# Attention scores of a state-space layer: from four fp32 products a batch to split fp32r products of 256 columns

## The reference

```python
B_ssm = ssm_in[..., :64]; C_ssm = ssm_in[..., 64:128]
# per token t and head: h = exp(d_t*A)*h + X_t * (d_t*B_t);  y_t = h . C_t
```

## Time and profile before

| | us |
|---|---|
| median of 3 runs (1521.78 to 1521.9) | 1521.87 |
| the profiled execution | 1522.09 |
| its span in the trace | 1520.4 |
| TensorE busy | 1504.6 (99%) |
| VectorE, GpSimd, ScalarE busy | 1128.1, 655.8, 606.0 |

### The profile page before, as it was taken

The page is one execution under the profiler, slowest core; times in us unless marked ns, Lnnn a source line. Parts: engine busy times, 40 slices in busy tenths (PEclk is TensorE's granted clock), DMA queues, the critical chain, the costliest instruction groups (busy, mean ns, idle before and its releaser), DMA issues.

```text
span 1520.4 us, 25377 instructions
## 1 busy us (share of the span) xinstructions
PE 1504.6 (99%) x8630; PEld 1250.7 (82%) x8630; DVE 1128.1 (74%) x3186; ACT 606.0 (40%) x1376; POOL 655.8 (43%) x747
## 2 busy tenths in 40 slices
PE   8999999999999999999999999999999999999998
PEld 7778888888888878888888888888888888888876
DVE  7797676967768677686876769777686776868755
ACT  6752424425244351533525244252443515335130
POOL 6771634616245270643606346162451715436040
PEclk9999999999999999999999999999999999999999
DMA  5350312314023040321404123140231403214020
GB/s 170 109 162 22 121 41 68 102 29 138 17 80 92 28 139 15 105 72 46 122 14 125 45 65 105 29 131 24 74 95 30 139 15 99 77 42 125 18 77 7
DMA packets 81505, 114.55 MB, mean 75 GB/s; under 512 B 10168, under 2 KB 37344, under 8 KB 81376
## 3 DMA queue, kind: packets, MB, share of 16 engines
q1 hardware_dynamic: 81376, 112.93, 24.6%
HBM read 107.77 MB, written 5.13 MB: 74 GB/s over the span
## 4 chain that ended last, share of the span: by engine, by line
PE 93%; POOL 2%; DVE 2%; DMA 1%; issue 1%; ACT 0%; SPq 0%; POOLq 0%; DVEq 0%; ACTq 0%
PE exp_bank L253 23%; PE exp_bank L255 22%; PE exp_bank L254 22%; PE mix_bank L964 4%; PE mix_bank L920 4%; PE mix_bank L253 3%; PE mix_bank L255 3%; PE mix_bank L254 3%; PE mix_bank L933 3%; PE mix_bank L814 1%; PE mix_bank L545 1%; PE mix_bank L762 1%; PE mix_bank L1056 1%; PE mix_bank L524 0%; POOL Wt L881 0%
## 5 line engine op out<-in xcount | busy, mean ns | idle before, releaser
L1241 POOL TENSOR_TENSOR sp_lo<-fbuf,sp_hi 128x512 fp32r<-128x512 f32 (+2 forms) x201 | 243.2, 1214 | 169.5 <-ACT sp_hi L1237 104.2
L253 PE MATMUL exp_bank<-w_hi,sp_hi 128*128 128x512 f32 x768 | 303.9, 396 | 1.2 <-POOL sp_lo L1294 0.8
L253 PE MATMUL exp_bank<-sp_hi,w_hi 128*128 128x512 f32 x764 | 302.8, 396 | 0.8 <-POOL sp_lo L1241 0.7
L255 PE MATMUL exp_bank<-w_hi,sp_lo 128*128 128x512 f32 x768 | 299.8, 390 | 0.0
L254 PE MATMUL exp_bank<-w_lo,sp_hi 128*128 128x512 f32 x768 | 299.0, 389 | 0.0
L255 PE MATMUL exp_bank<-sp_hi,w_lo 128*128 128x512 f32 x764 | 297.8, 390 | 0.0
L254 PE MATMUL exp_bank<-sp_lo,w_hi 128*128 128x512 f32 x764 | 297.5, 389 | 0.0
L1345 DVE SCALAR_TENSOR_TENSOR acc<-exp_bank,dw,acc 128x128 f32<-128x128 f32 x384 | 132.4, 345 | 163.6 <-PE exp_bank L255 162.8
L1237 ACT CAST sp_hi<-fbuf 128x512 fp32r<-128x512 f32 (+2 forms) x203 | 120.0, 592 | 270.7 <-DVE fbuf L1207 214.5
L881 POOL TENSOR_TENSOR Wt<-Wt,Gh 128x512 f32<-128x512 f32 x128 | 185.3, 1449 | 29.9 <-DVE Wt L870 29.9
L579 POOL TENSOR_TENSOR delta<-delta,bias_b 128x32 f32<-128x32 f32 x16 | 4.0, 253 | 414.3 <-ACT delta L555 409.2
(11 more groups left out here) (276 smaller groups left out, 2228.1 us busy)
## 6 DMA issues: line engine op xcount, KB each, us to landing
row_b<-dw_rows SPq DMA_DIRECT2D x189, 256.0 KB, 3.3
seg_b<-dA_rows SPq DMA_DIRECT2D x125, 256.0 KB, 3.4
ctd<-cum_rows SPq DMA_DIRECT2D x128, 96.0 KB, 3.2
x_in<-in_x SPq DMA_DIRECT2D x16, 256.0 KB, 2.7
result<-acc SPq DMA_DIRECT2D x15, 256.0 KB, 2.2
fbuf<-in_W1T SPq DMA_DIRECT2D x12, 256.0 KB, 4.0
acc<-in_W2T SPq DMA_DIRECT2D x4, 256.0 KB, 3.5
x_in<-in_W2T SPq DMA_DIRECT2D x4, 256.0 KB, 2.8
```

The lines of the kernel that those rows point to most:

```text
L253: nc.tensor.matmul(ps, s_hi, m_hi, start=start and j == 0, stop=False, skip_group_check=onto)
L255: last = nc.tensor.matmul(ps, s_lo, m_hi, start=False, stop=stop and j == n - 1, skip_group_check=onto)
L1241: sig("xw_lo", on.tensor_tensor(lo[:, cols], wide[e % 2][:, cols], hi[:, cols].bitcast(F32), ALU.subtract))
```

## The change

From batch 2 on, the scores are computed from split halves. The high half of B (rows 0 to 63) and its low half (rows 64 to 127) are stacked in one tile BS; CS holds the high half of the doubled C and, side by side, its low half. One fp32r product per chunk with K = 128 and 256 columns gives (B_hi+B_lo) C_hi and (B_hi+B_lo) C_lo in two column halves, which VectorE adds while it reads them from PSUM (`tensor_reduce`). BS and CS lie in the memory of zg.

The scores are made in two uses of a bank, two chunks each: the first behind transpose and sums, the second behind the third of the four column blocks of `expert_in(p, 0)`. The order of uses from batch 2 on is X0, X1, rates, G01, G23, X2, zg0 and so on, 25 a batch: G01 waits for the copy of X1, G23 for "ends", X2 and zg0 for VectorE's two sums. ScalarE's copy of the scores goes; its copy of B goes to BS; it makes C's high half behind tanh, and GpSimd C's low half behind the early part of the split. VectorE makes B's low half behind C's copies. The running product comes behind both sums on VectorE, where it was behind the end-sum reduction.

```diff
+MIX_LATER = (
+    MIX_USES[:MIX_USE["G"]] + [("rates", "ends", 1), ("G01", "Gm2", 1), ("G23", "Gm2", 2)] + MIX_USES[MIX_USE["X2"]:]
+)
+MIX_LATER[MIX_USE["BC"]] = ("BC", "B_lo", 1)
...
+        BS = nc.alloc_sbuf_tensor_at("BS", [P, T], F32R, offset=zg_at)
+        CS = nc.alloc_sbuf_tensor_at("CS", [P, 2, T], F32R, offset=zg_at + 4 * T)
...
 mix_bc:
-                AC.copy(BT[0:NS, :], bank_of("BC", b)[0:NS, :])
+                if later(b):
+                    wait(AC, "ps_out", b.prev())
+                    sig("B_hi", AC.copy(BS[0:NS, :], bank_of("BC", b)[0:NS, :]))
+                else:
+                    AC.copy(BT[0:NS, :], bank_of("BC", b)[0:NS, :])
...
+            if eng is DVE and later(b):
+                wait(DVE, "BC", b)
+                wait(DVE, "B_hi", b)
+                sig("B_lo", DVE.tensor_tensor(BS[NS:2 * NS, :], bank_of("BC", b)[0:NS, :], BS[0:NS, :].bitcast(F32), ALU.subtract))
+
+        def mix_c_split(eng, b):
+            if eng is AC and later(b):
+                wait(AC, "BC", b)
+                wait(AC, "ps_out", b.prev())
+                sig("C_hi", AC.copy(CS[:, 0, :], CT[:, :]))
+            if eng is PO and later(b):
+                wait(PO, "C_hi", b)
+                sig("C_lo", PO.tensor_tensor(CS[:, 1, :], CT[:, :], CS[:, 0, :].bitcast(F32), ALU.subtract))
...
+        def mix_scores_half(eng, b, n):
+            use, cs = f"G{2 * n}{2 * n + 1}", slice(2 * n, 2 * n + 2)
+            if eng is PE:
+                wait(PE, "B_lo", b)
+                wait(PE, "C_lo", b)
+                ps = mix_bank(b, use)
+                for j in range(2):
+                    at = tok(2 * n + j)
+                    last = PE.matmul(ps[:, 2 * j * P:2 * (j + 1) * P].rearrange("p (k t) -> p k t", k=2), BS[:, at], CS[:, :, at],
+                                     start=True, stop=True)
+                sig("ps_G2", last)
+            if eng is DVE:
+                wait(DVE, "ps_G2", b, n + 1)
+                wait(DVE, "G_dt", b.prev())
+                sig("Gm2", DVE.tensor_reduce(Gm[:, cs, :], bank_of(use, b)[:, :].rearrange("p (c k t) -> p c t k", c=2, k=2), AX.X, ALU.add))
...
 body:
             if norm_before:
                 expert_split(eng, p, 0, [1])
-                mix_scores(eng, b)
                 mix_silu_split(eng, b)
                 mix_rates(eng, b)
                 mix_ends(eng, b)
+                mix_scores_half(eng, b, 0)
+                if eng is DVE:
+                    mix_scores_half(DVE, b, 1)
+                    mix_running_product(b)
...
-                expert_in(eng, p, 0)
+                expert_in(eng, p, 0, lambda hc: hc == 2 and mix_scores_half(PE, b, 1))
...
                 mix_z(eng, nxt)
                 if eng is AC:
+                    mix_c_split(AC, nxt)
                     AC.preload_act_table_set(LOG_EXP)
             expert_row(eng, b, 0)
             expert_split(eng, b, 0, [0])
+            if front_next and eng is PO:
+                mix_c_split(PO, nxt)
```

More of the change, by code:

```diff
@@ L47 @@
 MIX_USE = {u[0]: n for n, u in enumerate(MIX_USES)}
+MIX_LATER = (
+    MIX_USES[:MIX_USE["G"]] + [("rates", "ends", 1), ("G01", "Gm2", 1), ("G23", "Gm2", 2)] + MIX_USES[MIX_USE["X2"]:]
+)
+MIX_LATER[MIX_USE["BC"]] = ("BC", "B_lo", 1)
+LATER_USE = {u[0]: n for n, u in enumerate(MIX_LATER)}
 MIX_FIRST = (
@@ L194, in layer_program @@
         product("G_skip", H, 1, 1)
+        for name, n in dict(ps_G2=2, Gm2=2, B_hi=1, B_lo=1, C_hi=1, C_lo=1).items():
+            product(name, n, 1, 2)
         product("xw", E, less=2)
@@ L271, in mix_bank @@
             for i in range(max(b.off - 1, 0), b.off + 1):
-                for u in MIX_USES if i else MIX_FIRST:
+                for u in MIX_LATER if i >= 2 else MIX_USES if i else MIX_FIRST:
                     if (i, u[0]) == (b.off, use):
@@ L289, in first, with later @@
             return b.reg is None and b.off == 0
+        def later(b):
+            return b.off >= 2
         def bank_of(use, b):
@@ L688, in mix_zg @@
                     wait(AC, "ps_out", b.prev())
+                    wait(AC, "ps_G2", b)
                     sig("zg", AC.copy(zg[:, q, :], bank_of(f"zg{q}", b)[:, :]))
@@ L708, in mix_rates @@
                 sig("end_sum", DVE.tensor_reduce(a_sums[:, :, :, :].rearrange("p k c h -> p k (c h)"), parts, AX.X, ALU.add))
-                wait(DVE, "rates_out", b.prev())
-                sig("ecum", DVE.tensor_tensor_scan(cum_t[R1, :], dA_t[R1, :], one[R1, :].to_broadcast([H * NC, P]),
-                                                   1.0, ALU.mult, ALU.mult))
+                if not later(b):
+                    mix_running_product(b)
             if eng is SP:
@@ L717, in mix_rates, with mix_running_product @@
                     start_rows(eng, b)
+        def mix_running_product(b):
+            wait(DVE, "dA", b)
+            wait(DVE, "rates_out", b.prev())
+            sig("ecum", DVE.tensor_tensor_scan(cum_t[R1, :], dA_t[R1, :], one[R1, :].to_broadcast([H * NC, P]),
+                                               1.0, ALU.mult, ALU.mult))
         def rates_out(b, part):
@@ L836, in mix_score_step @@
             if eng is AC:
-                wait(AC, "Gm", b)
+                wait(AC, "Gm2" if later(b) else "Gm", b)
                 if h >= 2:
@@ L1176, in route_rows @@
                 wait(AC, "dw_out", b.prev())
-                sig("dwT", AC.copy(rows[0:E * NC, :], bank_of("dwT", b)[0:E * NC, 0:P]))
+                owner = b if first(b) else Batch(b.reg, b.off + 1)
+                sig("dwT", AC.copy(rows[0:E * NC, :], bank_of("dwT", owner)[0:E * NC, 0:P]))
                 wait(AC, "ps_b2", b.prev())
-                sig("dw3T", AC.copy(bias_rows[:, :, :], bank_of("dwT", b)[:, 0:2 * P].rearrange("p (x t) -> p x t", x=2)))
+                sig("dw3T", AC.copy(bias_rows[:, :, :], bank_of("dwT", owner)[:, 0:2 * P].rearrange("p (x t) -> p x t", x=2)))
             if eng is SP:
@@ L1242, in expert_split, with expert_in @@
                                                   ALU.subtract))
-        def expert_in(eng, b, e):
+        def expert_in(eng, b, e, behind=lambda hc: None):
             if eng is PE:
@@ L1261, in expert_in @@
                         sig("ps_h_full", last)
+                    behind(hc)
                 if e < E - 1:
@@ L1852, in layer_program @@
         for p in prods.values():
-            written = 1 if p.name.startswith("end") and p.start else 3 if p.name != "x_in" else 2
+            written = 1 if p.name.startswith("end") and p.start else 3 if p.name not in ("x_in", "ps_G", "Gm") else 2
             count = p.done + p.less
```

6 lines of the change are left out of this document (5 added, 1 removed).

## The result

The changed kernel takes **1534.36 us** (median of 5 runs, 1533.88 to 1536.87) against 1521.78 for the kernel before in the same comparison (5 runs, 1521.27 to 1521.9). The ratio is 1.0086, with a 95% interval of 1.0073 to 1.01: 12.6 us slower, 0.90 us for each of the 14 batches. The forecast was 1535.8. The profiled execution took 1533.88 us, with a span of 1532.1.

A forecast was written before the change was run, and what follows sets the result against it. TensorE, busy 1504.6 of 1520.4 us, was taken as the bound. Terms 0.24 + 0.20 + 0.35 + 0.20 = 0.99 us a batch, x 14 = 13.9 us, gave 1535.8 us from 1521.87; range 1525.2 to 1542.2.

The forecast's parts named there:

- rival C: Ahead of expert 0: TensorE's own queue holds expert 0, so the kernel gets faster, 1516.1 us; chance 0.05.
- The hole's idle time: TensorE ahead of expert 0, held by casts and subtraction: 0.6 us becomes idle, removing scores there gains 0.
- Second pair: Score products of chunks 2 and 3, inside expert 0 in a TensorE stream without holes: +0.24 us a batch.
- Rival D: 256-column fp32r products cost twice 0.12 us each, so the second pair costs 0.24 more: 1539 us; chance within the forecast's 0.58.
- Step 2: Second pair waits for the ends, as GpSimd's earlier silu subtraction holds VectorE's accumulator add: +0.20 us a batch.
- Step 3: VectorE's reductions and held running product delay X2's copy, whose bank zg1 reuses: +0.35 us a batch.
- Step 4: SyncE's later cumulative-row store delays expert 3's row, so GpSimd's split collides with a state product: +0.20 us a batch.
- Rival A: Only the second pair is exposed: no VectorE-GpSimd collision, expert 3's row absorbed; 1525.6 us, chance 0.22.

The follow-up runs named there:

- experiments 1 and 3: 1: changed kernel, first pair of score products issued three times, 1537.21 us; 3: kernel before, scores of chunks 2 and 3 left out from batch 2, 1521.88 us.
- the run with both edits: Changed kernel with GpSimd's first silu subtraction waiting for VectorE's accumulator add, and the running product ahead of the score reductions: 1524.54 us.
- Experiment 2: Changed kernel with the second pair of score products, the one inside expert 0, issued three times: 1549.7 us.
- the fastest version: Changed scores, X2 and first pair ahead of expert 0, GpSimd waiting for the add, expert 3's row issued earlier, second reduction before expert 1's weighting: 1517.85 us.

## Why the prediction was right, and where not

**The sum.** 13.9 us forecast, 12.6 measured. The batches came out at 93.3 us where about 93.4 was said, and rival C (faster) fell with experiments 1 and 3: half the scores taken out of the hole is worth 0.07 us a batch, and expert 0 starts at the same distance from the last combine product with three times the pair in it. The hole's idle time, 0.56 us, was put at 0.6.

By the traces the 0.90 us a batch are the second pair 0.20, the ends 0.31, zg1 0.17 and the late splits 0.21, where 0.24, 0.20, 0.35 and 0.20 were forecast. Every term is there, but that the sum is off by 0.09 only is in part luck: the second term is 0.11 too small and the third 0.18 too large.

The forecast's times are in the kernel before's, where expert 0's first product starts at 713.16; in the changed kernel it starts at 717.50, so 4.34 is added to them below.

**Second pair, 0.24 us.** In the stream it takes 0.23 (716.93 to 717.16 in the run with both edits), and a batch without TensorE's waits is 0.18 to 0.21 longer, since expert 0's load also starts 0.03 us earlier than before. Right. The estimate of 0.22 by the Trainium skill's TensorE: Matmul & The Clock Gate (Back-to-back issue gap, 262 cycles for 256 columns) is as near. Rival D needed 0.48.

**Step 2, the ends, 0.20 us.** Right in its mechanism, 0.11 short. The add was to end 0.15 us behind GpSimd and did, and the pair came 0.21 us after its turn (719.91 against 719.70). What the term lacked was the restart behind an idle gap, another 0.10 us. It also holds a slip: 715.5 less 715.25 is 0.25, not 0.20; step 3 builds on it and would have been smaller by the same 0.05, so the sum is unchanged. And no row shows the 0.15 us that a released load was given; here the loads start 0.05 us behind what released them (719.44 + 0.42 = 719.86, 719.91). SBUF — State Buffer (Trainium skill, SBUF: two separate sides) says that a VectorE operation with two SBUF inputs and a GpSimd operation that reads SBUF exclude each other for a whole instruction; the 1.17 and 1.38 us of the add, and 28 reductions from PSUM at 0.69 beside GpSimd, agree.

**Step 3, X2's copy and zg1, 0.35 us.** The right wait at the right place, but half its size, 0.17 us. VectorE's side came out almost to the hundredth: the running product ended at 721.81 (forecast 717.47 + 4.34) and the copy of X2 at 723.00 (718.7 + 4.34 = 723.04). That the product took 0.75 us and not about 1 changes nothing here: it began later and ended where GpSimd let it. What was off is TensorE's side. Its turn came at 723.00 (721.64 + 2 x 0.68) instead of 718.48 + 4.34 = 722.82, mostly because of the restart that step 2 lacked, and the load followed the copy by 0.05 us instead of 0.15. So it started 0.05 us late, not 0.35, and the restart made that 0.17. Experiment 2, where VectorE arrives later against GpSimd, shows the other side of it, a product of 1.27 us.

**Step 4, SyncE's queue, 0.20 us.** The store of the cumulative row was to come 1.6 us later and did (721.95 against 715.99 + 4.34). In the batches from 2 on the late splits grew from 0.9 to 3.9 us, 0.21 a batch; moving the product ahead took them all away and gave back 2.9 us, 0.21 a batch. Right.

**What the steps left out.** As a list of what each wait costs, the steps add up. As a list of what can be mended, they mislead: one wait on GpSimd undid steps 2 and 3 together, 0.51 us a batch (7.2 / 14), and with the product's order it was 0.70 (9.8 / 14); the product's order alone, which was to cure step 3, only gave zg1's wait another name.

Rival A (only the pair exposed, 1525.6) is what the kernel comes to once both orders are made: 1524.54. Its condition, that VectorE and GpSimd don't meet, is not what makes it so: they still meet, at the running product's 1.29 us. It is enough that no wait of TensorE hangs on it.

## What to carry to other kernels

Work in a stretch that another chain keeps open is free to keep, and removing it gains nothing by itself: it makes room. The place to look is the work just behind that could be moved in, and it pays as far as it fits. Here a pair of 0.24 us brought quiet batches back to 92.44 us, and X2's 0.68 us brought them to 92.10; where the old scores had left no room, the same move of X2 gained nothing. So add up what the stretch holds, from the rows of the very kernel that is changed, before something is moved into it. When an edit takes an operation off one engine, the next ones on that engine start earlier, and that can put them in front of an operation of another engine that they exclude; look at what the freed engine now starts first, and make the order with a wait where it matters. Before mending waits one by one, ask whether one cause lies behind several of them, and try that first. And a hold in the trace is no loss by itself: in the fastest version the running product is still held for 1.47 us.

## What was not expected of the hardware

A hold between VectorE and GpSimd depends on which of them begins first, and its price jumps: the same add took 0.29 us when it went first and 1.38 when GpSimd had started 0.06 us ahead of it. In the rows looked at, the held operation ended 0.15 to 0.29 us behind GpSimd's instruction, wherever in it it had begun. So the running product of 32x128 took 0.40 us free, 0.75 when it met the later half of a scaling, 1.27 when it met one at its start and 1.46 when it began 0.11 us into a silu subtraction. And a wait of TensorE costs about 0.1 us more than its lateness: behind an idle gap the second product follows the first after 0.34 us (717.50, 717.84) instead of 0.23.
